# Moving the second group sums, the eps spread and the second expert matrices in a graph-layer kernel

## The reference

```python
h = logmap0(proj(x, c), c)
h = batchnorm(conv1d(h, w_qkv), bn_gamma, bn_beta)     # 768 channels: q, k, v
t = logmap0(proj(proj(expmap0(relu(h), c), c), c), c)
s = conv1d(conv1d(t, w_dw, groups), w_pw, groups)      # 32x32 blocks
t2 = logmap0(proj(expmap0(concatenate([t, s]), c), c), c)
q, k, v = split(t2)                                    # q and k through relu
vk = einsum("ngdl,ngel->ngde", v, k)
out = einsum("ngde,ngdl->ngdl", vk, q) / (sum(v, -1) + ATT_EPS)
ft = conv1d(logmap0(proj(expmap0(out, c), c), c), w_res) + b_res
fx = proj(expmap0(ft, c), c)
x = x + gnn + fx
x = x + ffn(layernorm(x))     # y = sum over 2 chosen experts of gelu(x W1 + b1) W2 + b2, then a norm
```

## Time and profile before

| what | us |
|---|---|
| median of three runs | 843.91 |
| profiled execution | 845.02 |
| its span | 843.2 |
| PE busy in the span | 789.9 (94%) |
| DVE, ACT, POOL busy | 523.4, 424.6, 389.2 |
| PE busy of the 140 us from 260 to 400 (in the mixer's steps) | 138.42 |
| DVE, ACT, POOL busy in the same stretch | 118.01, 120.33, 116.61 |
| PE busy of the 80 us from 400 to 480 | 62.00 |
| PE busy of the 333 us from 510 to 843 (experts) | 326.63 |

### The profile page before, as it was taken

The page is one execution under the profiler, slowest core; times in us unless marked ns, Lnnn a source line. Parts: engine busy times, 40 slices in busy tenths (PEclk is TensorE's granted clock), DMA queues, the critical chain, the costliest instruction groups (busy, mean ns, idle before and its releaser), DMA issues. The chain is left out here.

```text
span 843.2 us, 15014 instructions
## 1 busy us (share of the span) xinstructions
PE 789.9 (94%) x5042; PEld 648.9 (77%) x5042; DVE 523.4 (62%) x1475; ACT 424.6 (50%) x959; POOL 389.2 (46%) x601
## 2 busy tenths in 40 slices
PE   5899999999799999999659889999999999999996
PEld 4678888888466667766436778888888888888885
DVE  7762488797578888788888643534444353535345
ACT  2466436889578888888647232323232323222230
POOL 2430778778068888887636601312222221312122
PEclk9899999999899999999969999999999999999999
DMA  9755122222011110211101040000000000000000
GB/s 213 192 152 152 40 58 56 55 52 52 8 48 43 55 57 25 64 42 51 45 7 33 19 125 13 17 21 22 16 25 13 24 13 25 13 25 14 25 20 30
DMA packets 35422, 41.32 MB, mean 49 GB/s; under 512 B 11520, under 2 KB 20696, under 8 KB 35339
## 3 DMA queue, kind: packets, MB, share of 16 engines
q1 hardware_dynamic: 22355, 30.71, 12.8%
q0 software_dynamic: 8000, 6.82, 3.8%
q10 hardware_dynamic: 4984, 2.79, 1.4%
HBM read 25.59 MB, written 14.60 MB: 48 GB/s over the span
## 5 line engine op out<-in xcount | busy, mean ns | idle before, releaser
L916 ACT ACTIVATE Z<-ps,b1s 128x250 f32<-128x250 f32 x200 | 93.5, 469 | 234.9 <-PE ps L1182 232.1
L1195 PE MATMUL ps<-Z 128*125 128x256 f32 x800 | 176.5, 379 | 0.0
L1182 PE MATMUL ps<-Z 128*128 128x250 f32 x800 | 173.6, 374 | 2.3 <-DMA Z<-in_w 2.3
L1195 PEld LDWEIGHTS ps<-Z 128*125 128x125 f32 x800 | 150.2, 188 | 22.2
L1182 PEld LDWEIGHTS ps<-Z 128*128 128x128 f32 x800 | 151.3, 189 | 20.5 <-DMA Z<-in_w 2.9
L978 PE MATMUL ps<-Z,L 128*128 128x250 f32 x600 | 126.9, 373 | 0.0
L651 POOL TENSOR_SCALAR zr<-zmv 125x1 f32<-125x1 f32 x50 | 11.1, 221 | 250.1 <-issue 240.3
L978 PEld LDWEIGHTS ps<-Z,L 128*128 128x128 f32 x600 | 113.6, 189 | 13.2
L1770 DVE TENSOR_TENSOR Z<-ps,L 125x256 f32<-125x256 f32 x50 | 21.2, 425 | 161.1 <-PE ps L1195 161.1
L1097 PE MATMUL ps<-wr,Z 128*125 128x256 f32 x400 | 92.6, 384 | 0.0
L774 ACT ACTIVATE Z<-Z,bn_o,bn_s 128x250 f32<-128x250 f32 x150 | 80.8, 600 | 1.5 <-DVE bn_o L1481 1.5
(11 more groups left out here) (214 smaller groups left out, 1287.7 us busy)
## 6 DMA issues: line engine op xcount, KB each, us to landing
Z<-in_x SPq DMA_DIRECT2D x25, 250.0 KB
out<-Z SPq DMA_DIRECT2D x24, 250.0 KB
xt_table<-L SPq DMA_DIRECT2D x25, 231.0 KB
Z<-in_x SPq DMA_DIRECT2D x1, 2016.0 KB
g_table<-gt SPq DMA_DIRECT2D x25, 62.5 KB
gr<-g_table SPq DMA_DIRECT2D x25, 62.5 KB
Z<-in_x SPq DMA_DIRECT2D x1, 1344.0 KB
Z<-in_w SPq DMA_DIRECT2D x2, 512.0 KB, 3.4
```

Of the source, the lines that this page charges most:

```text
L916: a_.activation(ge[:, b % 2, f, :], ps[:, f % 4, 0:BT], ACT.Gelu, bias=b1s[:, f // NF, f % NF:f % NF + 1]).then_inc(gelu_done.sem, 1)
L1182: last = mm(ps[:, f % 4, 0:BT], w1s[:, f // NF, k, (f % NF) * 128:(f % NF + 1) * 128], h_of(b, k), start=(k == 0), stop=(k == KD - 1))
L1195: last = mm(ps[0:TP, 4 + 2 * (b % 2) + t, 0:D], ge[:, b % 2, f, t * TP:(t + 1) * TP], w2s[:, f // NF, f % NF, :], start=(f == 0), stop=(f ...
```

## The change

Five things change. (1) `k_sums_s` uses all four quarters: the first half goes to bank 1, the second to bank 2, so s of v moves from bank 2 into the upper halves of banks 3 and 4, and the k channels of the second half keep their order; for that the preparation uses smaller pieces (ACT 8 instead of 4 at L759, DVE 24 instead of 12 at L1349). (2) `turn_xn` stands behind `k_sums_s` and ahead of `norms`. (3) On DVE `attend_s` stands ahead of `check_s` and `attend_t`, and the next `pointwise_kq` waits for it, since it reads banks 1 and 2. (4) In the division, eps is spread over wider tiles with one copy, one transpose and 6 copies instead of 1, 1 and 16, and the second half's quotients are moved by 2 copies more. (5) The first expert's w2, b2 and what follows them on SP are issued when the second expert's w1 has landed.

```diff
@@ load_expert
             eng.dma_start(b1s[:, i, :], b1[e].rearrange("(k p) -> p k", p=128),
                           allow_slow_non_contiguous=True).then_inc(b1_in[i], 16)
+            if i == 0:
+                eng.wait_ge(w1_in[1], 16)
             eng.dma_start(w2s[:, i, :, :], w2[e].rearrange("(k p) f -> p k f", p=128)).then_inc(w2_in[i], 16)
@@ square_s (ACT)
-                a_.activation(sqs[:, r], ps[:, r, 0:2 * BT], ACT.Square).then_inc(s_sq.sem, 1)
+                if r == R_V:
+                    act.wait_ge(kst_done.sem, kst_done.count(b))
+                    a_.activation(pair(sqs[:, r]), ps[:, 3:5, BT:2 * BT], ACT.Square).then_inc(s_sq.sem, 1)
@@ pointwise_kq (PE)
+                    pe.wait_ge(att.sem, att.count(b - 1, 1))
@@ pointwise_v (PE)
-                    pe.wait_ge(att.sem, att.count(b - 1, 1))
+                    pe.wait_ge(att.sem, att.count(b - 1, 2))
...
-                        last_v = quarter(bank_half(R_V, h), pw[:, cv, :], zc(b, cv), a, a)
-                        last_k = quarter(bank_half(3, h), bo, zc(b, ck), a, 1 - a)
+                        last_v = quarter(bank_half(4 - h, 1), pw[:, cv, :], zc(b, cv), a, a ^ h)
+                        last_k = quarter(bank_half(3 + h, 0), bo, zc(b, ck), a, 1 - (a ^ h))
@@ k_sums_s (PE)
-                for h in range(NH):
-                    for a in range(2):
-                        last = quarter(bank_half(4, h), bo, skr[:, h * BT:(h + 1) * BT], a, a)
-                last.then_inc(kss_done.sem, 1)
+                for a in range(2):
+                    last_0 = quarter(bank_half(1, 0), bo, skr[:, 0:BT], a, a)
+                    last_1 = quarter(bank_half(2, 0), bo, skr[:, BT:2 * BT], a, 1 - a)
+                last_0.then_inc(kss_done.sem, 1)
+                last_1.then_inc(kss_done.sem, 1)
@@ steps (PE)
-                (4, turn_xn),
                 (0, pointwise_v),
                 (0, k_sums_s),
+                (4, turn_xn),
                 (0, norms),
@@ divide_where_needed (DVE)
-                    alone(v_.tensor_copy(ebt[0:TP, 0], et[0:TP, 2].rearrange("p (t a) -> p t a", a=1).broadcast_to([TP, TB, 32])))
-                    alone(v_.transpose(ebt[:, 1].rearrange("p t c -> p (t c)"), ebt[:, 0].rearrange("p t c -> p (t c)")))
-                    for q in range(4):
-                        w = min(32, TP - 32 * q)
-                        for p in range(4):
-                            alone(v_.tensor_copy(eb.rearrange("p (t n) -> p t n", t=TB)[32 * p:32 * p + 32, :, 32 * q:32 * q + w],
-                                                 ebt[32 * q:32 * q + 32, 1, :, 0:w]), q == 3 and p == 3)
+                    alone(v_.transpose(eb, den[:, 0:TB * 128]))
+                    places = eb.rearrange("p (t q c) -> p t q c", t=TB, q=4)
+                    alone(v_.tensor_copy(places[64:128, :, 0:2], places[0:64, :, 0:2]), False)
+                    alone(v_.tensor_copy(places[0:64, :, 2:4], places[64:128, :, 2:4]))
...
+                    alone(v_.tensor_copy(eb[0:HALF, 0:BT], vk[HALF:128, 0:BT]), False)
+                    alone(v_.tensor_copy(eb[HALF:128, 0:BT], vk[0:HALF, 0:BT]))
@@ steps (DVE)
                 (2, make_u),
+                (0, attend_s),
                 (0, check_s),
                 (0, attend_t),
-                (0, attend_s),
```

More of the change, by code:

```diff
@@ L172, in gps_layer @@
         zr = sb("zr", [128, 2, 2, 1])
-        LW = 9914
+        LW = 9920
         L = sb("L", [128, LW])
@@ L213, in gps_layer @@
         spill = take(D // 2).bitcast(BF16)
-        eb = take(BT)
+        eb = take(TB * 128)
         den = take(NH * BT)
@@ L379, in gps_layer @@
         xt_rows, g_rows = tok(xt_table), tok(g_table)
+        pair = lambda a: a.rearrange("p (h n) -> p h n", h=NH)
         WQ_IN, BN_IN, PW_IN, LATE = 16 * KD, 16 * 3, 16 * 16, 16 * 3
@@ L757, in _ @@
                     if r == R_K:
[L758 to L761, removed]
+                        for h in range(NH):
+                            for e in range(2):
+                                a_.activation(
+                                    wq[:, k, 256 * r:256 * r + 256].rearrange("p (h e q i) -> p h e q i", h=NH, e=2, i=GROUP)[:, h, e ^ 1 if h == 0 else e],
+                                    wq_raw(k).rearrange("p (h e q r i) -> p r h e q i", h=NH, e=2, r=3, i=GROUP)[:, r, h, e],
+                                    ACT.Copy).then_inc(wq_made, 1)
                     else:
@@ L1347, in _ @@
                     j = 3 * q + r
-                    p = q ^ 2 if r == R_K else q
-                    v_.tensor_copy(per3[32 * p:32 * p + 32, :, 2 * r:2 * r + 2],
-                                   raw3[32 * (j % 4):32 * (j % 4) + 32, :, j // 4:j // 4 + 4:3]).then_inc(permuted, 1)
-            dve.wait_ge(permuted, 12)
+                    for h in range(NH):
+                        p = q ^ 2 if r == R_K and h == 0 else q
+                        v_.tensor_copy(per3[32 * p:32 * p + 32, :, 2 * r + h],
+                                       raw3[32 * (j % 4):32 * (j % 4) + 32, :, j // 4 + 3 * h]).then_inc(permuted, 1)
+            dve.wait_ge(permuted, 24)
             dve.wait_ge(pw_in, PW_IN)
@@ L1500, in _ @@
             edge_sums(EARLY // 2 - 1)
-            pair = lambda ap: ap.rearrange("p (h n) -> p h n", h=NH)
             def keep_k(b):
@@ L1582, in divide_where_needed @@
-                    halves = ((zc(b, 2 * R_V, 2), den, ob(b, 0, 2)), (ps[:, R_V, 0:2 * BT], vk, ob(b, 2, 2)))
-                    for n, (v, d, _) in enumerate(halves):
-                        alone(v_.tensor_tensor(pair(d), pair(v), eb.rearrange("p (a n) -> p a n", a=1)
-                                               .broadcast_to([128, NH, BT]), ALU.add), n == 1)
-                    for n, (_, d, _) in enumerate(halves):
-                        alone(v_.reciprocal(d, d), n == 1)
-                    for n, (v, d, _) in enumerate(halves):
-                        alone(v_.tensor_tensor(d, v, d, ALU.mult), n == 1)
@@ L1590, in divide_where_needed @@
-                    for n, (_, d, o) in enumerate(halves):
-                        alone(v_.tensor_tensor(o, o, d, ALU.mult), n == 1)
+                    alone(v_.tensor_copy(den[0:TP, 0:TB * 128].rearrange("p (t n) -> p t n", t=TB),
+                                         et[0:TP, 2].rearrange("p (t a) -> p t a", a=1).broadcast_to([TP, TB, 128])))
+                    alone(v_.transpose(eb, den[:, 0:TB * 128]))
+                    places = eb.rearrange("p (t q c) -> p t q c", t=TB, q=4)
+                    alone(v_.tensor_copy(places[64:128, :, 0:2], places[0:64, :, 0:2]), False)
@@ new lines, in divide_where_needed @@
+                    halves = ((tokens(zc(b, 2 * R_V, 2)), den), (ps[:, 3:5, BT:2 * BT].rearrange("p h (t n) -> p h t n", t=TB), vk))
+                    for n, (v, d) in enumerate(halves):
+                        alone(v_.tensor_tensor(tokens(d), v, eps, ALU.add), n == 1)
+                    for n, (_, d) in enumerate(halves):
+                        alone(v_.reciprocal(d, d), n == 1)
+                    for n, (v, d) in enumerate(halves):
+                        alone(v_.tensor_tensor(tokens(d), v, tokens(d), ALU.mult), n == 1)
```

28 lines of the change are left out of this document (19 added, 9 removed).

## The result

The changed kernel takes 835.3 us (median of 8 runs, 833.6 to 840.1) against 843.4 us (8 runs, 840.9 to 846.7): a ratio of 0.991, with a 95% interval of 0.989 to 0.993, 8.1 us less. One of the 12 executions of experiment 4 took 4634.6 us; it counts in no ratio. The profiled execution took 833.7 us with a span of 831.9. That is 11.3 less than the profiled one of before, and 2.7 of it lies in front of the mixer, where the first `pointwise_kq` starts at 204.71 instead of 207.43.

What follows compares the result with a forecast made beforehand. Two chains of nearly one length were taken to bound the mixer, PE's 9.19 us and the ring's mean of about 9.2. 845.0 - 1.2 - 1.0 - 0.9 - 2.0 + 0.1 = 840.0, said as 839.0 on the median's scale; range 833 to 843.

Steps and rivals of the forecast that it cites:

- PE paces all steps: Rival, mixer: the ring mostly runs at 8.84 us, so PE saves 0.32 in 25 steps; 833 us, chance 0.15.
- terms 1 and 2: PE's mixer step: four-quarter sums save 0.42 us, moved transposes cost a switch of about 0.1; 9.19 becomes 8.87.
- The cover of the transposes: PE, mixer: transposes ahead of `norms` make it wanted 1.94 us behind `pointwise_v`'s start; without them 1.4 and it waits.
- The ring: Mixer chain from `make_x1` through DVE, ACT and POOL to the next `make_x1`: 8.84 or 9.53 us, mean about 9.2.
- term 3: Mixer steps 2 to 21, with gather pieces: the ring stays, PE waits for `fixed`; 0.06 a step, -1.2 us.
- PE's waits at L998: Sign in the profile after: PE waiting 0.2 to 0.6 us there in most steps, ended by `fixed`.
- term 4: Three steps behind the gather, without gather piece: PE sets their pace, 3 x 0.32, -1.0 us.
- term 5: Division in one block: 16 copies become six wider ones, other copies grow; -0.9 us, bounds 0.4 and 1.5.
- term 6: Experts' start: w2 issued later, so the second expert's w1 lands earlier and PE's wait goes; -2.0 us.
- term 7: Preparation: four ACT activations at L759 become eight narrower, DVE gets 12 more small copies; +0.1 us, up to 1.
- The wait for `attend_s`: Mixer, PE's next `pointwise_kq`: `attend_s` ends at 352.6, PE gets there at 353.0; margin 0.4 us, costs nothing.
- the ring gives nothing: Rival, mixer: L1600 misses the gap in L595 in more steps; 841 to 842 us on the median's scale, chance 0.27.

Runs made afterwards that it cites:

- experiment 4: Changed kernel with the second group sums on two quarters of the array again: ratio 0.9993 to the kernel before, median 843.7 us, 9.42 us a step.
- experiment 3: Changed kernel with the transposes back in their old place ahead of `pointwise_v`: ratio 0.9946 to the kernel before, median 838.6 us, 9.32 us a step.
- Experiment 5: Changed kernel with `check_s` behind `attend_t` on DVE instead of ahead of it: ratio 0.9934 to the kernel before, median 837.2 us, 9.27 us a step.
- experiment 7: Changed kernel with the exponential of the late graph edges behind ACT's relus: ratio 0.9871 to the kernel before, median 832.8 us, 9.03 us a step.
- experiment 6: Changed kernel with the second instruction of `attend_t`, the product, behind `make_xn` on DVE: ratio 0.9908 to the kernel before, median 835.8 us.
- experiment 1: Kernel before plus one line: the first expert's second matrix issued when the second expert's w1 has landed. Ratio 0.9970 to the kernel before, median 841.8 us.
- experiment 10: Kernel before with only the exponential of the late graph edges moved behind ACT's relus: ratio 0.9974 to the kernel before, median 839.7 us.
- experiments 2: Changed kernel without the load wait ahead of the first expert's second matrix: ratio 0.9939 to the kernel before, median 837.4 us.
- experiment 8: Changed kernel with POOL's gather piece ahead of the edge additions: ratio 0.9941 to the kernel before, median 838.0 us, 9.28 us a step.

## Why the prediction was right within its range, and wrong in a step

The direction was right, and 835.3 lies inside the range of 833 to 843. But it lies outside the forecast's own 837 to 841, nearer to the 833 of the rival "PE paces all steps": 8.1 us were saved, 4.9 forecast. One step failed, others were mis-sized.

**PE's step** (terms 1 and 2) was right in its parts. The sums save 0.42 by the rows (0.45 by experiment 4). The move costs: `pointwise_kq` to `pointwise_v` without the transposes grows by 0.09 us, the transposes by 0.05. So 8.92 instead of the forecast 8.87; for the extra switch I had 0.1, the move costs 0.14 by the rows and 0.19 by experiment 4. The cover of the transposes was needed, as said: without it all that the steps gained is lost again (experiment 3). The Trainium skill (TensorEngine Tiling (Array Packing), Key Properties), which says that a change of tiling mode drains the engine, agrees with the 0.14 to 0.19 us, and the cost was outweighed by the waits of 0.42 us at `norms` that the cover avoids.

**The ring** (term 3) is the step that failed: "the ring stays", and with it the 1.2 us. I had its length from the rows and assumed that nothing in it changes, because the change touches no instruction of it. But the order on DVE (part 3 of the change) moved a product off POOL's power, and the ring's two lengths fell from 8.84 and 9.53 to 8.52 and 9.2. With that the ring's fast steps are below PE's 8.92 and the slow ones only 0.3 above it, so that PE sets most of the pace; this is why PE's waits at L998, announced as the sign, are missing. Experiment 5 gives the ring its old length and shows what term 3 would have been: 9.27 a step against 9.33 before, 0.06 x 16 = 1.0 us, the 0.06 a step that I had worked out, and waits of PE at L998 in 7 of 15 steps. The shorter ring added 0.1 a step, 1.7 us. What keeps the changed kernel's mean at 9.16 and not at 8.92 is mostly ACT's late square in every fourth step, which experiment 7 removed (9.03) and no term had. The rival "PE paces all steps" was thus half true, but not for the reason given for it, an earlier L1600: as L1624 of the changed kernel it still took 0.34 us or more in 13 of 15 steps, and POOL's power is what became shorter.

The stall has a rule in the Trainium skill (SBUF — State Buffer, Who interferes with whom): a DVE instruction with two inputs in SBUF contends with a GpSimd instruction that reads SBUF, and the order of issue decides which of them blocks. The traces agree on the contention: `Z<-L,Z` lengthened the power from 0.71 to 1.22 us in two kernels and L612 from 0.2 to 0.85 in a third, while `attend_s`, which has one input in PSUM, passed beside POOL without a stall. The gather piece is no exception: it took 1.56 us where the product began 0.33 us ahead of it (experiment 6). L1600, which waits behind POOL's additions (0.71 us), is the same thing the other way round. Which of two comes first can't be read from the starts of the rows alone: in experiment 6 L612 begins 0.13 us ahead of the product and still ends with it, and in the changed kernel the product begins 0.15 us before the power ends and takes its usual 0.68.

**Behind the gather** (term 4): 0.6 measured, 1.0 forecast. PE's steps there are 8.92 too; one late square on ACT remains (0.62 us of wait at `norms`).

**The division** (term 5) was sized nearly right: DVE's part is 1.15 us shorter, and PE's wait 15.46 - 14.24 = 1.2, instead of 0.9. I had charged 0.2 us each for the wider copy and transpose and 0.35 for each of two more copies. The wider copy and transpose took 0.29 and 0.45 in all (0.20 and 0.24 before), the two copies 0.29 and 0.28, and the six copies 0.22, 0.63 and 0.97 for the last four. The other 0.6 of the stretch's 1.7 lies behind the division, from PE's first matmul to `make_x1`, 8.61 before and 8.02 after; the same stretch took 7.88 in experiment 1 and 9.11 in experiment 10, which have the program of before there, so it can't be put down to the change.

**The second matrices** (term 6): 2.3 measured against 2.0 between the two profiles; the line alone gives 1.7 and 0.8 in the traces of experiments 2 and 1. **The preparation** (term 7): no cost to be seen, but the start of the mixer varies by up to 4 us, in which 0.1 or even 1 us would hide. **The wait for `attend_s`** (8): PE did not wait for it in the steady steps. **The rival "the ring gives nothing"** has a slip in its sum: 843.0 to 841.5 is 841.9 to 840.4 on the median's scale, not 841 to 842; nothing hangs on it.

The terms together, as measured in the stretches (2.1 + 1.7 + 0.6 + 2.3), are 6.7 us of the 8.1. The rest would lie in the first steps of the mixer, where the three profiles without the change differ by 3.7 us (33.5, 34.4 and 37.2), and stays open.

## What to carry to other kernels

Where two chains of nearly one length lie beside each other, look at the order of every engine that the change touches, not only at its instructions: one that moved can hold up or free another engine. Before a saving on one engine is counted, find the periodic late step of the others; moving one small exponential that waited for DVE in every fourth step gave 3.4 us here by the ratios and 3.0 in the trace (`make_x1` 0 to 18), more than several parts of the change. Look at the rare steps too: the order of experiment 8, chosen for the steady steps, cost 1.5 us on DVE in the one block that divides. Work that fills a wait, as the transposes do, is worth its price in mode switches only where the wait is there, and putting it back is the shortest test.

## What was not expected of the hardware

- POOL's power of 125x2 takes 0.71 us, 1.22 when a DVE product of two SBUF tiles begins 0.04 us ahead of it, and 0.87 to 0.89 beside `make_xn` (one SBUF input, float32).
- POOL's gather piece takes 1.35 us, 1.56 when the same product begins 0.33 us ahead of it; a DVE copy of 64x128 takes 0.22 us, 1.76 when it begins 0.45 us behind the start of a gather piece that POOL's additions follow.
- One load of 512 KB, issued at the same place of the program, landed 4.5 to 7.0 us later in kernels that differ only far from it.
- The start of the program, up to the mixer, took 204.7 to 205.5 us in some profiles and 206.9 to 208.5 in others, for the kernel before and the changed one alike.
